# Joining LayerNorm's even and odd statistics with bn_aggr, and another order of work, in a transformer block kernel

## The reference

```python
qkv = einsum('btc,ec->bte', x, Wqkv) + bqkv          # 256 -> 768
q, k = elu(q * scale) + 1, elu(k * scale) + 1        # 16 heads of 16
kv = k * v
y = q * cumsum(kv) / clip(sum_d(q * cumsum(k)), 1e-3)
x = layernorm(x + y @ Wproj.T + bproj)
h = gelu(block_quant(x) @ block_quant(w_fc).T + b_fc)        # 256 -> 1024
x = layernorm(x + block_quant(h) @ block_quant(w_proj).T + b_proj)
```

## Time and profile before

| | us |
|---|---|
| median of 3 runs | 281.32 (280.38 to 281.45) |
| the profiled execution's own time | 282.59 |
| its span, first to last instruction | 280.8 |
| TensorE busy | 252.6 (90%) |
| VectorE busy | 243.3 (87%) |
| GpSimd busy | 169.9 (60%) |
| ScalarE busy | 168.8 (60%) |

### The profile page before, as it was taken

How to read it: one execution, slowest core, us unless ns; L and a number is a source line. 1 busy time by engine, 2 the same in 40 slices (tenths; PEclk the granted TensorE clock), 3 DMA queues, 4 the chain that set the end, 5 groups by cost and what they waited for, 6 DMA issues and landing times.

```text
span 280.8 us, 4189 instructions
## 1 busy us (share of the span) xinstructions
PE 252.6 (90%) x1476; PEld 158.1 (56%) x1476; DVE 243.3 (87%) x505; ACT 168.8 (60%) x278; POOL 169.9 (60%) x113
## 2 busy tenths in 40 slices
PE   5798998999999999999999999999999998858650
PEld 4545553665575656675676557655766565633330
DVE  2289788989899989999899989998999999987941
ACT  0563426757669576848676856866694766345712
POOL 1056365666856594777568666759565947763831
PEclk9799799999999999999999999999999999999995
DMA  6930020002001300030002200220001000200202
GB/s 162 363 76 2 0 75 2 0 2 75 0 2 49 103 1 1 2 120 30 2 0 75 78 1 0 77 75 0 2 25 50 4 0 0 77 1 0 75 2 75
DMA packets 13556, 11.82 MB, mean 42 GB/s; under 512 B 3040, under 2 KB 13280, under 8 KB 13536
## 3 DMA queue, kind: packets, MB, share of 16 engines
q1 hardware_dynamic: 11904, 11.28, 12.5%
q10 hardware_dynamic: 1632, 0.27, 0.6%
HBM read 7.35 MB, written 4.19 MB: 41 GB/s over the span
## 4 chain that ended last, share of the span: by engine, by line
DVE 51%; PE 34%; POOL 4%; ACT 3%; issue 3%; DMA 3%; ACTq 1%; POOLq 0%; DVEq 0%
PE abank L964 19%; DVE h_amax L748 11%; DVE stats L722 7%; DVE kvsum L700 6%; DVE hq L659 5%; PE dbank L1028 4%; DVE y L712 3%; DVE r L716 3%; DMA Wproj_sb<-in_L_attn_Wproj_dram 3%; DVE h_pow L651 2%; PE tbank L1021 2%; PE bbank L996 2%; DVE kv L690 2%; DVE r L760 2%; PE hbank L1014 2%
## 5 line engine op out<-in xcount | busy, mean ns | idle before, releaser
L964 PE MATMUL abank<-xT,WqkvT 128*128 128x512 f32 x176 | 85.3, 609 | 0.8 <-ACT xT L429 0.8
L323 POOL TENSOR_TENSOR h_round<-h,h_inv 128x1024 f16<-128x1024 f32 x32 | 73.7, 2302 | 16.2 <-DVE h_inv L654 16.2
L964 PEld LDWEIGHTS abank<-xT,WqkvT 128*128 128x128 f32 x176 | 30.5, 192 | 24.3 <-issue 22.3
L444 ACT ACTIVATE h<-hbank 128x512 f32<-128x512 f32 x64 | 36.4, 593 | 9.6 <-PE hbank L1014 9.2
L438 ACT ACTIVATE expz<-abank,zbias_neg 128x512 f32<-128x512 f32 x30 | 20.6, 687 | 32.4 <-PE abank L964 32.1
L748 DVE TENSOR_REDUCE h_amax<-h 128x32 f32<-128x1024 f32 x32 | 38.7, 1209 | 1.2 <-ACT h L444 1.2
L1014 PE MATMUL hbank<-w_fcT,xqT 128*128 128x512 bf16 x128 | 38.1, 379 | 0.0
L308 POOL TENSOR_TENSOR rstd<-vareps,minus_half 128x4 f32<-128x4 f32 x16 | 18.4, 1151 | 32.4 <-DVE vareps L734 32.4
L1028 PE MATMUL dbank<-w_prT,hT 128*128 128x256 bf16 x256 | 33.3, 273 | 3.6 <-ACT hT L454 3.6
L299 POOL TENSOR_TENSOR qk<-qf,ksum 128x512 f32<-128x512 f32 x16 | 22.0, 1379 | 20.8 <-DVE qf L683 17.2
L303 POOL TENSOR_TENSOR num<-qf,kvsum 128x512 f32<-128x512 f32 x16 | 27.2, 1715 | 10.4 <-DVE kvsum L700 10.4
(11 more groups left out here) (100 smaller groups left out, 409.9 us busy)
## 6 DMA issues: line engine op xcount, KB each, us to landing
x_sb<-in_L_attn_x_dram SPq DMA_DIRECT2D x8, 512.0 KB, 3.6
out_dram<-o_sb SPq DMA_DIRECT2D x7, 512.0 KB, 2.9
h<-in_L_ffn_w_fc_dram SPq DMA_DIRECT2D x1, 1024.0 KB, 10.9
h<-in_L_ffn_w_proj_dram SPq DMA_DIRECT2D x1, 1024.0 KB, 12.6
Wqkv_sb<-in_L_attn_Wqkv_dram SPq DMA_DIRECT2D x1, 512.0 KB, 6.6
out_dram<-o_sb SPq DMA_DIRECT2D x4, 128.0 KB, 1.7
Wqkv_sb<-in_L_attn_Wqkv_dram SPq DMA_DIRECT2D x1, 256.0 KB, 7.7
Wproj_sb<-in_L_attn_Wproj_dram ACTq DMA_DIRECT2D x1, 256.0 KB, 7.9
```

Source lines behind the costliest of these rows:

```text
L323: nc.gpsimd.tensor_tensor(h_round[:, t % 2].rearrange("p (g j) -> p g j", j=BLOCK_K), h[:, t].rearrange("p (g j) -> p g j", j=BLOCK_K), h_ ...
L444: nc.scalar.activation(h[:, t, half * HALF:(half + 1) * HALF], hbank[half][:, :], ACT.Gelu).then_inc(s_h, 1)
L964: last = nc.tensor.matmul(ps[:, :], WqkvT[:, k, e * P:(e + 1) * P], xT[:, k], start=(k == 0), stop=(k == CC - 1))
```

## The change: what it does

It has two parts. The first is in `mean_var`: after the four `bn_stats`, four `bn_aggr` (one per tile) turn each tile's even and odd statistics into a mean and a variance, and two small operations make the negated mean and the variance plus epsilon. The tile `mv` changes its shape to suit.

The second part is another order of calls in the lists of every engine, in the start, the steps and the end. SyncE's list loses the semaphore `out_buffer_free` and its own wait after each store; `norm_2` waits for the store itself. The instructions outside `mean_var` are the same ones.

```diff
-        mv1 = sb("mv1", [P, 4, TILES])
+        mv1 = sb("mv1", [P, TILES, 2])
...
-            def store(S, b, R):
-                wait(sp, s_o, S + 1)
-                sp.dma_start(out_d[b, bass.ds(R, 1)].rearrange("o p t c -> (o p) t c"), o_sb[:, :, :]).then_inc(s_out, 16)
-                wait(sp, s_out, 16 * S + 16)
-                sp.sem_inc(s_ofree, 1)
...
+            def store(n):
+                wait(sp, s_o, n + 1)
+                sp.dma_start(out_d[n % 2, n // 2], o_sb[:, :, :]).then_inc(s_out, 16)
...
@@ GpSimd, step @@
                 q_times_kvsum(n, n % 2, 0)
+                n = s
+                scale_shift_2(n)
+                n = s + 2
                 q_times_kvsum(n, n % 2, 1)
-                n = s
-                scale_shift_2(n)
...
@@ ScalarE, norm_2 @@
                 wait(act, s_sh2, S + 1)
-                wait(act, s_ofree, S + 1)
+                wait(act, s_out, 16 * S)
...
@@ ScalarE, end @@
             gelu(7, 1, 1)
+            norm_2(6)
             gelu(7, 2, 0)
-            norm_2(6)
             gelu(7, 2, 1)
+            gelu(7, 3, 0)
             copy_hT(7, 0)
-            gelu(7, 3, 0)
...
@@ VectorE, mean_var @@
                 last.then_inc(s_st, 1)
-
                 wait(dve, s_st, S + 1)
-                mean_e, m2_e, mean_o, m2_o = (stats[:, :, n] for n in (1, 2, 4, 5))
-                nc.vector.tensor_tensor(mv[:, 0], mean_e, mean_o, ALU.add)
-                nc.vector.tensor_tensor(mv[:, 1], mean_e, mean_o, ALU.subtract)
-                nc.vector.scalar_tensor_tensor(mv[:, 2], m2_e, C * LN_EPS, m2_o, ALU.add, ALU.add).then_inc(s_mv, 1)
-                wait(dve, s_mv, 2 * S + 1)
-                nc.vector.tensor_scalar(negmean[:, :], mv[:, 0], -0.5, None, ALU.mult)
-                nc.vector.scalar_tensor_tensor(mv[:, 3], mv[:, 1], 0.25, mv[:, 1], ALU.mult, ALU.mult).then_inc(s_mv, 1)
-                wait(dve, s_mv, 2 * S + 2)
-                nc.vector.scalar_tensor_tensor(vareps[:, :], mv[:, 2], 1.0 / C, mv[:, 3], ALU.mult, ALU.add).then_inc(s_ve, 1)
+                for t in range(TILES):
+                    last = nc.vector.bn_aggr(mv[:, t], stats[:, t])
+                last.then_inc(s_mv, 1)
+                wait(dve, s_mv, S + 1)
+                nc.vector.tensor_scalar(negmean[:, :], mv[:, :, 0], -1.0, None, ALU.mult)
+                nc.vector.tensor_scalar(vareps[:, :], mv[:, :, 1], LN_EPS, None, ALU.add).then_inc(s_ve, 1)
...
@@ VectorE, step @@
             def step(s):
+                n = s + 1
+                mean_var_1(n)
                 n = s
                 h_exponents(n, 3)
-                n = s + 1
-                mean_var_1(n)
-                n = s
                 quantise_h(n, 2)
                 residual_2(n, n % 2, 0)
                 n = s + 2
                 feature(n, 1, 0, abank[0])
+                n = s
+                residual_2(n, n % 2, 1)
+                n = s + 2
+                feature(n, 0, 0, abank[1])
                 sum_k(n, n % 2, 0)
-                feature(n, 0, 0, abank[1])
-                n = s
-                residual_2(n, n % 2, 1)
+                n = s
+                quantise_h(n, 3)
                 n = s + 2
                 multiply_kv(n, 0, abank[0])
                 n = s + 1
                 x_exponents(n, n % 2)
-                n = s
-                quantise_h(n, 3)
-                n = s + 2
+                n = s + 2
+                sum_kv(n, n % 2, 0)
                 feature(n, 1, 1, abank[1])
                 n = s
                 residual_2(n, n % 2, 2)
                 n = s + 2
+                feature(n, 0, 1, abank[0])
+                n = s + 1
+                quantise_x(n)
+                n = s + 2
                 sum_k(n, n % 2, 1)
-                n = s + 1
-                quantise_x(n)
-                n = s + 2
-                feature(n, 0, 1, abank[0])
                 multiply_kv(n, 1, abank[1])
-                sum_kv(n, n % 2, 0)
+                n = s
+                residual_2(n, n % 2, 3)
+                mean_var_2(n)
+                n = s + 2
+                denominator(n)
                 sum_kv(n, n % 2, 1)
-                n = s
-                residual_2(n, n % 2, 3)
-                n = s + 2
-                denominator(n)
-                n = s
-                mean_var_2(n)
...
@@ TensorE, step (only what moves against its neighbours) @@
                 project(n, 1, 0, abank[0])
-                wait(pe, s_hT, 4 * n + 1)
-                transpose_hq(n, 1)
                 down(n, 0)
...
-                wait(pe, s_r2, 4 * n + 2)
-                down(n, 2)
...
                 project(n, 0, 1, abank[0])
+                n = s
+                down(n, 2)
...
                 denominators(n)
+                n = s + 1
+                up(n, 0, 1)
+                n = s + 3
+                transpose_x(n, n % 2, 0, abank[0])
...
                 project_out(n, 0)
+                n = s + 1
+                transpose_hq(n, 0)
+                n = s + 2
+                project_out(n, 1)
+                n = s + 1
+                wait(pe, s_h, 8 * n + 6)
+                up(n, 3, 1)
+                wait(pe, s_hT, 4 * n + 1)
+                transpose_hq(n, 1)
```

More of the change, by code:

```diff
@@ L265, in _ @@
[L265 to L285, removed]
+            def load_bias_rows():
+                sp.wait_ge(s_bsplit, 5)
+                sp.wait_ge(s_rows0, 1)
+                for r in range(3):
+                    sp.dma_start(bias_rows[r:r + 1, 0:HID], b_part[:, r, 0:HC]).then_inc(s_brow, 16)
+                    sp.dma_start(bias_rows[r:r + 1, HID:HID + C], b_part[:, r, HC:HC + CC]).then_inc(s_brow, 16)
+                    sp.dma_start(bias_rows[r:r + 1, HID + C:], b_part[:, r, HC + CC:]).then_inc(s_brow, 16)
@@ L287, in _, with step @@
+            load_bias_rows()
+            load(2)
+            def step(s):
+                n = s + 3
+                load(n)
+                n = s
+                store(n)
+            for s in range(STEPS):
+                step(s)
+            store(5)
+            store(6)
+            store_last(7)
         @block.gpsimd
@@ L550, in step @@
                 gelu(n, 0, 0)
+                gelu(n, 0, 1)
                 n = s + 2
@@ L577, in _ @@
                 step(s)
+            gelu(5, 3, 1)
+            activate(7, 1, 0, abank[0])
             activate(7, 0, 0, abank[1])
@@ L586, in _ @@
             gelu(6, 0, 0)
+            gelu(6, 0, 1)
             widen_rec(7)
-            gelu(6, 0, 1)
             gelu(6, 1, 0)
@@ L857, in step @@
                 n = s + 2
+                attention_out(n, 0)
                 attention_out(n, 1)
@@ L871, in _ @@
                 step(s)
+            mean_var_1(6)
             h_exponents(5, 3)
-            mean_var_1(6)
             quantise_h(5, 2)
@@ L877, in _ @@
             feature(7, 1, 0, abank[0])
+            residual_2(5, 1, 1)
+            feature(7, 0, 0, abank[1])
             sum_k(7, 1, 0)
-            feature(7, 0, 0, abank[1])
-            residual_2(5, 1, 1)
+            quantise_h(5, 3)
             multiply_kv(7, 0, abank[0])
             x_exponents(6, 0)
-            quantise_h(5, 3)
+            sum_kv(7, 1, 0)
             feature(7, 1, 1, abank[1])
             residual_2(5, 1, 2)
+            feature(7, 0, 1, abank[0])
+            quantise_x(6)
             sum_k(7, 1, 1)
-            quantise_x(6)
-            feature(7, 0, 1, abank[0])
             multiply_kv(7, 1, abank[1])
-            sum_kv(7, 1, 0)
+            residual_2(5, 1, 3)
+            mean_var_2(5)
+            denominator(7)
             sum_kv(7, 1, 1)
-            residual_2(5, 1, 3)
-            denominator(7)
-            mean_var_2(5)
+            h_exponents(6, 0)
             attention_out(7, 0)
-            h_exponents(6, 0)
             attention_out(7, 1)
@@ L1098, in _ @@
             up(0, 0, 0)
-            pe.wait_ge(s_w16, 4)
+            pe.wait_ge(s_kv, 4)
+            transpose_x(2, 0, 1, abank[1])
+            denominators(1)
             up(0, 0, 1)
-            denominators(1)
             pe.wait_ge(s_h, 1)
@@ L1164, in step @@
                 n = s + 1
-                up(n, 0, 1)
-                n = s + 3
-                wait(pe, s_kv, 2 * n)
-                transpose_x(n, n % 2, 1, abank[1])
-                n = s + 1
                 wait(pe, s_h, 8 * n + 1)
                 up(n, 1, 0)
+                wait(pe, s_h, 8 * n + 2)
+                up(n, 1, 1)
                 n = s + 2
@@ L1183, in step @@
                 up(n, 2, 1)
+                n = s + 3
+                transpose_x(n, n % 2, 1, abank[1])
+                n = s + 1
                 wait(pe, s_h, 8 * n + 5)
```

105 lines of the change are left out of this document (48 added, 57 removed).

## The result

The changed kernel takes **287.66 us** (median of 4 runs, 286.72 to 288.34), against 281.38 for the kernel before in the same series (280.38 to 283.59). The ratio is 1.021, 95% interval 1.0139 to 1.028: slower, as forecast (the interval does not settle whether by more or less than 2%), and inside the range, by 0.14, but 3.2 above the 284.5 that was forecast. Medians here are over all runs; ratios leave out a run over 1.5% above the fastest of its kernel. The profiled execution took 287.04, its span is 285.2; before it was 282.59 and 280.8. The sum is judged on the 4.45.

A forecast was written before the change was run, and what follows sets the result against it. The prediction took a loop through both TensorE and VectorE as the bound. Steps +3.9, start -0.2 and end -0.5 summed to +3.2, giving 284.5 us against the median of 281.32, with a range from 280.6 to 287.8.

The forecast's parts named there:

- (a): Loop part from `quantise_h(n, 1)` to the second `down`: 5.88 before and 5.88 forecast after.
- (b): Loop part in which VectorE's `residual_2(n, 1)` waits for the second `down` to end, 0.99 plus 0.2 hand-over: 1.2.
- (c): VectorE's calls from `residual_2(n, 1)` to the start of `sum_k(x, 1)`: 8.7, and 8.8 with `round_x` some 0.1 late.
- (d): Scan of the keys 1.28, GpSimd's product 1.27 and two hand-overs at about 0.14, until `denominators` starts: 2.8.
- (e): TensorE from `denominators` to the end of `project_out(x, 0)`, same calls as before: 9.44.
- (f): From the end of `project_out(x, 0)` to `quantise_h(u, 1)`, through `residual_1` and exponents, same calls as before: 2.46.
- the dear case of 0.19: In `mean_var`, `bn_aggr` cannot overlap its neighbour and costs 0.19 each: +2.6, 287.1; a dear `bn_aggr` had chance 0.12.
- The start: Many small swaps before the steps, `gelu(0, 0)` earlier and `up(0, 0, 1)` later: -0.2, with 0.5 either way.
- The end: After the steps: both `mean_var` of chunk 7 on the chain, -0.22, and `norm_2(6)` moved up, -0.3; together -0.5.
- TensorE alone as the bound: Rival: the key-sum wait doesn't come and TensorE runs at 29.3 a step, about 277.2; chance of faster 0.12.
- waits that only change places: Rival: no change, the loop stays at 29.9 to 30.1, 281 to 282.5; chance 0.16.
- the loop as walked: Main case in the steps: loop of 30.6 a step, +3.9 over the six; own range 283.0 to 286.0, chance 0.60.

The follow-up runs named there:

- experiment 1: The kernel before with only the new `mean_var`, in the old order of calls: 279.74 us, ratio 0.9929.
- experiment 8: experiment 1's kernel with `norm_2(6)` ahead of `gelu(7, 2, 0)` and `gelu(7, 3, 0)` ahead of `copy_hT(7, 0)` at ScalarE's end: 279.91 us, ratio 0.9952.
- experiment 9: experiment 3's kernel with ten 256-column matmuls, results not read, in TensorE's wait in front of `denominators`: 288.6 us, ratio 1.0237.
- 12: experiment 1's kernel, with TensorE made to wait for `residual_2(n, 3)` before `denominators(x)` in the five steps: 299.76 us, ratio 1.0642.
- experiment 6: The changed kernel with VectorE's steps in the order of before, all other lists as changed: 297.45 us, ratio 1.0584.
- 7: experiment 1's kernel with VectorE's steps in the new order, all other lists as before: 289.62 us, ratio 1.0286.
- experiment 5: The changed kernel with TensorE's `up(u, 0, 1)` put in front of `denominators(x)` again: 284.73 us, ratio 1.0139.
- experiment 3: The changed kernel with `sum_kv(x, 0)` moved behind `sum_k(x, 1)` on VectorE: 300.37 us, ratio 1.0641.

## Why the prediction was right, and where it was off

- **The bound** (a loop through TensorE and VectorE, cut at `quantise_h(n, 1)`) held. The chain after has one period of 30.41 in all undisturbed steps, in two profiles of the same kernel.
- **The walk.** The parts, forecast and measured: (a) 5.88 and 5.87; (b) 1.2 and 1.20 (130.87 to 132.07); (c) 8.8 and 8.62 (to 140.69); (d) 2.8 and 2.74 (to 143.43); (e) 9.44 and 9.51 (to 152.94); (f) 2.46 and 2.47. Sum 30.6 and 30.41. Nearly all of the 0.17 is (c). In it `sum_kv(x, 0)` took 1.19 (137.07 to 138.26) and not 1.40, the half of a pair whose first scan had taken 1.62 (139.45 to 141.07) and shared its first 0.6 with GpSimd's product; and `round_x` came 0.2 late, not 0.1. Sums of prices read from start to start of the same call, before, carried over to another order within some 2%; a single price was off by 15%.
- **A slip in the sum.** Five times 30.6 and 30.2 are 183.2, not the 183.4 written down; the term should have read +3.7. Measured 182.03: the other 1.2 is 0.2 a step. And before, no step is shorter for want of the next transposes: the sixth takes 29.87 like the others, and the mean of 29.92 comes from the fourth.
- **The waits.** In front of `denominators` 0.44, not 0.9, ended by GpSimd's qk as forecast; at the second `down` 0.21 from start to start (1.93 from 128.94 to 130.87, where the same call takes 1.72), of which the profile prints none, not 0.3; VectorE in front of `residual_2(n, 1)` 0.50, not 0.65. The first was worked out as 12.8 less 11.93, both from the second `down`; measured, the way is 12.56, and TensorE needs 0.19 more than before for the calls between (12.12, from 130.87 to 142.99), so that the wait shrinks from both sides.
- **`bn_aggr`.** 0.10, 0.07 and 0.07 from start to start, 0.08 on average, as taken; the dear case of 0.19 is out. With one wait for two, `mean_var` is 0.14 shorter; 0.11 was forecast. The rule that only the count of operations matters, six for six, would have made experiment 1 no faster at all; it was 0.7% faster. The 67 ns that the prediction estimated from the Trainium skill ("VectorE: DVE Perf Modes", section "The TRN2 errata") agree with the two starts that are 0.07 apart; one `bn_aggr` by itself is busy for 157 ns.
- **The start** gave -0.4 for -0.2, inside the 0.5 either way. **The end** gave -0.2 for -0.5: `norm_2(6)`, for which -0.3 was taken out of 0 to -0.5, is worth 0 (experiment 8). The two `mean_var` there account for the rest.
- **The rivals.** TensorE alone as the bound (277.2) and waits that only change places (281 to 282.5) are out by the period. No listed case holds what happened in full: the loop as walked, and a second loss. That 287.66 lies inside the range at all is luck. The loop as walked had 283.0 to 286.0 for itself; what reaches from there to 287.8 was put there for a dear `bn_aggr`, which did not come, and took in a loss that nobody had counted.
- **The step that failed** is the sum: 3.9 - 0.2 - 0.5 has no term for TensorE's clock. The forecast named the wait ("a larger one for the key sums comes") and priced it as idle time. It did not ask what TensorE does on the far side of it: `denominators`, 1.8 us of matmuls with 8 columns. Idle and then so little work was followed, in two of six steps, by TensorE at 1.2 GHz, and cost 2.7 here, as much as the loop's own loss (2.5). The earlier trace rows gave a hint: clock 1.00 in the steps, 0.95 and 0.91 in the start and the end, where TensorE waits more.

That the waits in front of `denominators` bring the stretches is shown by experiments 9 and 12, and by the count behind 12. That it takes the 8-column matmuls too is not separated: experiment 6 speaks for it, but no run changes `denominators` itself. Open is also why one step has one and the next, with the same calls, has not; how much of the loss each single move of the order makes (experiments 6 and 7 show that the lists can't be taken one by one); and how far the start's own stretches make the spread between runs.

## What to carry to other kernels

Walk the loop of the new order with start-to-start prices from the trace before: here it gave the period to 0.6%. Then look at each new wait of TensorE and at what stands on both sides of it; one in front of a run of narrow matmuls can cost more in clock than in idle time, and filling it, best with real work moved up, is cheap. Take a change with two parts apart before you judge it: one part alone won 0.7%, the other alone lost 2.7%.

## What the runs showed of the hardware

- A wait of 0.44 us of TensorE in front of 1.8 us of 8-column matmuls was followed, in 7 of 24 steps, by a stretch at half clock, in which two `up` matmuls took 1.06 instead of 0.59. A wait of 1.3 in front of 256-column matmuls (experiment 6) was not, in six steps. The Trainium skill ("TensorE: Matmul & The Clock Gate", section "A second HAM failure mode: psum-queue depth-cycling") tells of a kernel in which frequent short pauses make the clock swing between its two levels. The traces here agree that short pauses can do it; here it was one of 0.44 at this place in a step of 30, and the kernel of experiment 5, which has that pause filled with an `up`, stayed at clock 1.00 through all six steps.
- Ten matmuls without use in each step made a kernel 11.8 us faster (experiment 9 against 3, medians).
- GpSimd's product of 128x512 takes 1.27 where no scan is running when it begins, and 2.10 beside a scan that VectorE had begun (experiment 3). In the kernel before, where the product began first (138.79) and the scan later (139.45), the product kept its 1.27 and the scan took 1.62 to the next one's start, where it takes 1.19 in the changed kernel. So "VectorE is free now" and "GpSimd is fast now" don't hold together.
- `bn_aggr` of 6 values shows 157 ns busy for one, and four in a row start 0.10, 0.07 and 0.07 apart.
